# A decoder layer on one core: maxima seven steps ahead of the scores, transposes moved with them

## The chip, the cores and the metric

The kernel runs on one core of a Trainium2 chip. Each of its engines works through its own queue in order: TensorE (PE, matmuls and weight loads), VectorE (DVE), ScalarE (ACT), GpSimd (POOL), and SyncE (SP), which here only issues DMAs. They wait for each other through semaphores. The metric is the device time of one execution in microseconds (us); lower is better.

## What is computed

The reference is one decoder layer on x of shape (8, 512, 256), with 16 heads of 16 features: self-attention with rotary embedding, cross-attention to a context of the same shape, and a mixture of experts, each with a residual sum and a layer norm behind it. Cut to what matters here:

```python
attn = jnp.einsum('bhtd,bhsd->bhts', q, k) * scale
attn = jax.nn.softmax(attn, axis=-1)
out = jnp.einsum('bhts,bhsd->bhtd', attn, v)
x = _layernorm(x + _L0_attn_ref(x, Wqkv, Wout))
x = _layernorm(x + _L0_xattn_ref(x, ctx, ctx, ...))
x = _layernorm(x + _L0_ffn_ref(x, ...))
```

The softmax needs the maximum of each query's scores before the exponential.

## The kernel before

The program has two phases, attention and then the mixture of experts (MoE). Only the attention phase is touched.

**Halves and steps.** For each batch element k (batch, from here on) there is a FIRST half, with the self-attention of batch k, and a SECOND half, with the cross-attention of batch k − 1. The 16 heads are four groups of four (NG = 4), and the 512 keys are four blocks (TT = 4). A half has 16 steps (STEPS): step s takes group s // 4 and block s % 4 of the keys. In a step TensorE does four scores (L721, `ps_sc`, keys on the partitions, queries along the row), four maxima products (L707, `ps_max`, queries on the partitions) for work that is some steps ahead, in the middle the outputs of the step before (`head_outputs`, L738, `ps_out`), and after the last of the four the step's jobs. ScalarE takes the exponentials of the scores (L478). VectorE takes the maxima (L520), negated, into `nm`, one column for each head and query block.

**How a maximum reaches the scores.** Sixteen columns of `nm` make a group. The job `nm0` g (self) or `nm1` g (cross) transposes them on TensorE (L693) into a job bank. ScalarE copies the high part to `mst` (L390), VectorE takes the difference as the low part (L502), and SP writes both by four DMAs into two rows of `qk` on the side of the queries (`mrows`, L229). There they meet rows of ones on the side of the keys, so the scores' product has the maximum already subtracted. The first score of group g, in step 4g, waits for these DMAs (`mrow_in`).

**What else runs in the steps.** The table TASKS gives, for each half and step, the jobs as (kind, number, offset of the batch): projections (`q`, `k`, `v` of the next self-attention, `cq`, `ck`, `cv` of the next cross-attention), transposes of outputs (`ot`, `nt`), output projections (`w0`, `w1`), layer norms (`ln0`, `ln1`), splits (`x`, `c`, `xt`). TensorE does a job at the end of its step; ScalarE and VectorE do their part of it at the start of the next step, VectorE ahead of that step's four maxima. The order inside a step is that of the list.

**Two job banks.** The jobs of TensorE share two PSUM banks in turn, by their place in ORDER, the list of all jobs of both halves. `free_bank` (L629) makes a job wait until the one two places ahead of it has been read out of its bank.

**How far ahead.** LEAD says how many steps the maxima run ahead of the scores. Near the end of a half they belong to the next attention:

```python
inst, first = (cur, TT * (s + LEAD)) if s + LEAD < STEPS else (nxt, TT * (s + LEAD - STEPS))
return [(inst, n) for n in range(first, first + TT)] if inst else []
```

```python
def bank(kind, n):
    return ps_job[:, [t[:2] for t in ORDER].index((kind, n)) % 2, :]
```

```python
at = [t[:2] for t in ORDER].index((kind, n)) - 2
...
pe.wait_ge(read[prev], upto(prev, b, m))
```

**SP's order.** `qk` holds one attention; group g of the next is loaded over it by twelve DMAs (`stack`, L258) when group g of the present one has its scores: for groups 0, 1 and 2 at the end of steps 4, 8 and 12, for group 3 at the start of the next half. The rows come from scratch in HBM: `hbm_ck` and `hbm_cq` are stored in step 3 of FIRST, when `ck` 1 and `cq` 1 are split, and `hbm_self` in steps 3 and 5 of SECOND. In a step SP first issues the `mst` DMAs of that step's `nm` job, then stores, then a `stack`.

Of the kernel before, what the change touches and what calls it, by code (L numbers as in the profile page):

```python
# [18 lines left out]
NG = H // HG  # L19
HM = H // FC  # L20
NSC, NMX = 2, 3
LEAD = 6
PV_AT = 2
JOB_AT = 3
STEPS = NG * TT
# [15 lines left out]
SELF, CROSS = 0, 1  # L41
TASKS = {
    FIRST: {
# [5 lines left out]
    },  # L49
    SECOND: {  # L50
# [5 lines left out]
    },  # L56
}

# [25 lines left out]
def attention_phase(nc, x, xT, cT, w_att, tables, b_cols, bo_rows, x2, hbm_self, hbm_ck, hbm_cq, slots_x, sums):  # L84
    with ExitStack() as ctx:
# [107 lines left out]
        def maxima_of(s, cur, nxt):  # L193

            inst, first = (cur, TT * (s + LEAD)) if s + LEAD < STEPS else (nxt, TT * (s + LEAD - STEPS))
            return [(inst, n) for n in range(first, first + TT)] if inst else []
# [1488 lines left out]
```

## Time and profile before

| | us |
|---|---|
| median of 3 runs | 1755.08 |
| lowest, highest of them | 1749.54, 1757.05 |
| the profiled execution | 1748.39 |
| its span, first to last instruction | 1746.6 |
| TensorE busy with matmuls | 1493.3 (85%) |
| VectorE, ScalarE, GpSimd busy | 1118.8, 913.1, 437.9 |
| mean granted TensorE clock | 0.855 |

The attention phase fills the span up to some 1290 us, MoE the rest. Busy time of TensorE is modelled at the ends of matmuls, so 85% is not 85% of its peak. The granted clock is a share of full speed: 1.00 is 2.4 GHz, 0.50 is 1.2 GHz, and a figure between them is a stretch that has both. In the timeline a row is a run of like instructions: start, length, engine, line, operation, output <- input, count, and in brackets the idle time of the engine before it and what ended that.

### The profile page before, as it was taken

What the parts mean: (1) busy time and instruction counts of PE and PEld (TensorE: products, weight loads), DVE (VectorE), ACT (ScalarE), POOL (GpSimd) and SP (SyncE); (2) the same over time, 40 slices, a digit from 0 to 9 for tenths busy, and PEclk for the clock granted to TensorE, in tenths of its full rate; (3) what the DMA queues carried; (4) which work ended last, traced back from release to release, by engine and by line L of the source; (5) the groups of instructions that cost most, each with busy time, mean ns of one, the idle gap of its engine ahead of it and who ended that gap; (6) DMA issues with size and microseconds to landing.
All of it is one profiled execution on the core that took longest, in us unless ns stands there. A gap on an engine that the chain in (4) does not pass through costs nothing. (4 is left out here: it accounts for less than half of the span.)

```text
span 1746.6 us, 27669 instructions
## 1 busy us (share of the span) xinstructions
PE 1493.3 (85%) x8424; PEld 872.5 (50%) x8424; DVE 1118.8 (64%) x2282; ACT 913.1 (52%) x1702; POOL 437.9 (25%) x411
## 2 busy tenths in 40 slices
PE   3887889989889898988997988886876889999994
PEld 2324334435444444443443533333235778999984
DVE  3716568778678678868877876835514754555556
ACT  3441556656556555655665665651533543555544
POOL 4004013013013003202301301001002543666664
PEclk8657879989888899999998988986557988999998
DMA  4213333333243234233323313204003533677672
GB/s 148 73 53 103 123 94 100 103 110 107 63 130 122 57 109 125 79 118 111 100 98 107 114 50 121 66 1 131 4 1 135 183 128 121 125 148 134 129 202 97
DMA packets 110136, 179.85 MB, mean 103 GB/s; under 512 B 20288, under 2 KB 65984, under 8 KB 107968
## 3 DMA queue, kind: packets, MB, share of 16 engines
q1 hardware_dynamic: 95424, 159.11, 29.3%
q0 software_dynamic: 14592, 19.41, 6.4%
q8 instruction: 42, 0.69, 0.2%
q14 instruction: 78, 0.64, 0.1%
HBM read 98.09 MB, written 79.30 MB: 102 GB/s over the span
## 5 line engine op out<-in xcount | busy, mean ns | idle before, releaser
L520 DVE TENSOR_REDUCE nm<-ps_max 128x1 f32<-128x512 f32 x1024 | 644.7, 682 | 212.3 <-PE ps_max L707 210.9
L478 ACT ACTIVATE prob<-ps_sc 128x512 f32<-128x512 f32 x1024 | 555.8, 596 | 398.2 <-PE ps_sc L721 396.3
L721 PE MATMUL ps_sc<-qk 50*128 50x512 f32 x1024 | 446.1, 520 | 118.4 <-DMA qk<-mst 97.9
L707 PE MATMUL ps_max<-qk 48*128 48x512 f32 x1024 | 466.5, 534 | 26.8 <-DVE nm L520 18.5
L721 PEld LDWEIGHTS ps_sc<-qk 50*128 50x128 f32 x1024 | 185.6, 212 | 479.2 <-ACT prob L478 279.2
L738 PE MATMUL ps_out<-prob,va 128*32 128x512 f32 x2048 | 327.8, 717 | 4.8 <-ACT prob L478 3.4
L707 PEld LDWEIGHTS ps_max<-qk 48*128 48x128 f32 x1024 | 190.8, 212 | 75.4 <-DVE nm L520 63.0
L1472 PE MATMUL ps_gu<-x2f,we 128*128 128x256 f32 (+1 forms) x1344 | 222.1, 320 | 4.6 <-ACT sg L1137 2.4
L1472 PEld LDWEIGHTS ps_gu<-x2f,we 128*128 128x128 f32 x1344 | 189.3, 191 | 21.9 <-DVE h L1363 3.1
L360 POOL TENSOR_TENSOR rstd<-mv,eps 128x2 f32<-128x2 f32 x32 | 6.3, 197 | 680.7 <-DVE mv L589 680.7
L1472 PE MATMUL ps_dn<-we,hf 128*128 128x256 f32 x864 | 123.1, 299 | 11.1 <-DVE totals L1446 10.5
L1472 PEld LDWEIGHTS ps_dn<-we,hf 128*128 128x128 f32 x864 | 117.1, 205 | 12.7 <-DVE hf L1367 12.1
L625 PE MATMUL ps_job<-xf,w 128*128 128x512 f32 x288 | 93.0, 467 | 21.8 <-POOL xf L335 16.7
L738 PEld LDWEIGHTS ps_out<-prob,va 128*32 128x32 f32 x2048 | 43.3, 115 | 99.1 <-issue 92.8
L625 PE MATMUL ps_job<-w,cf 128*128 128x256 f32 x576 | 84.6, 299 | 5.3 <-DVE cf L504 3.6
L1061 POOL DMA_INDIRECT slots_x<-x2in,scat x64 | 65.7, 1026 | 87.3 <-DVE tok L1353 29.5
L625 PEld LDWEIGHTS ps_job<-xf,w 128*128 128x128 f32 x288 | 60.5, 225 | 47.5 <-issue 29.0
L625 PEld LDWEIGHTS ps_job<-w,cf 128*128 128x128 f32 x576 | 75.5, 200 | 15.3 <-issue 8.8
L344 POOL TENSOR_TENSOR res<-res,trig 128x512 f32<-128x512 f32 x32 | 40.9, 1279 | 159.0 <-DVE res L537 159.0
L1075 POOL DMA_INDIRECT sums<-ys,dest x40 | 62.2, 1555 | 49.7 <-DVE dest L1404 26.4
L1075 POOL DMA_INDIRECT x<-ys,dest x40 | 62.1, 1552 | 31.3 <-ACT ys L1202 20.0
L335 POOL TENSOR_TENSOR xf<-raw,xf 128x1024 fp32r<-128x1024 f32 x8 | 19.1, 2389 | 163.1 <-ACT xf L390 163.1
(145 smaller groups left out, 1489.0 us busy)
## 6 DMA issues: line engine op xcount, KB each, us to landing
qk<-hbm_self SPq DMA_DIRECT2D x384, 64.0 KB, 2.3
hbm_self<-stage SPq DMA_DIRECT2D x16, 1024.0 KB, 3.9
qk<-hbm_cq SPq DMA_DIRECT2D x192, 64.0 KB, 2.4
qk<-hbm_ck SPq DMA_DIRECT2D x192, 64.0 KB, 2.3
slots_x<-zeros SPq DMA_DIRECT2D x8, 1360.0 KB, 5.8
xs<-slots_x SPq DMA_DIRECT2D x40, 272.0 KB
weraw<-w_moe SPq DMA_DIRECT2D x11, 768.0 KB
hbm_ck<-stage SPq DMA_DIRECT2D x8, 1024.0 KB, 4.3
```

Source lines behind the costliest of these rows:

```text
L335: nc.gpsimd.tensor_tensor(out, value, high.bitcast(F32), ALU.subtract).then_inc(lo_done[kind], 1)
L344: nc.gpsimd.tensor_tensor(rot[:, c, :], rot[:, c, :], trig[:, 1, :], ALU.mult) \
L360: nc.gpsimd.tensor_tensor(rstd[:, at, :], mv[:, at, 1:2], eps[:, at, :], ALU.add) \
L478: nc.scalar.activation(prob[:, s % 2, j, :], ps_sc[:, (HG * s + j) % NSC, :], ACT.Exp, scale=HD ** -0.5).then_inc(exp_done[a], 1)
L520: nc.vector.tensor_reduce(nm[:, g % 2, r:r + 1], ps_max[:, n % NMX, :], axis=AX.X, op=ALU.max, negate=True).then_inc(max_done[a], 1)
L625: ins = nc.tensor.matmul(out, l(a), r(b), start=(n == 0 and k == 0), stop=(n == len(pairs) - 1 and k == len(parts) - 1))
L707: nc.tensor.matmul(ps_max[:, n % NMX, :], qk[rows, 0, pair, P * c:P * c + P], qk[rows, 1, pair, :], start=True, stop=True).then_inc(smax_d ...
L721: nc.tensor.matmul(ps_sc[:, n % NSC, :], qk[rows, 1, h // 2, P * c:P * c + P], qk[rows, 0, h // 2, :], start=True, stop=True).then_inc(st_ ...
L738: ins = nc.tensor.matmul(ps_out[32 * j:32 * j + 32, :], va[:, a, c, HG * g + j, :], prob[:, s % 2, j, :], start=(c == 0), stop=(c == TT - ...
L1061: nc.gpsimd.indirect_dma_start(rows_x, bass.IndirectOffsetOnAxis(ap=scat[:, q, c, t:t + 1], axis=0), xin[:, q, t, :], None, bounds_check=P ...
L1075: nc.gpsimd.indirect_dma_start(x2 if j // NCH else sums, bass.IndirectOffsetOnAxis(ap=dest[:, c, t:t + 1], axis=0), ys[:, c, t, :], None, ...
L1472: ins = nc.tensor.matmul(o, l(a), r(b), start=(n == 0 and k == 0), stop=(n == len(pairs) - 1 and k == len(parts) - 1))
```

## The change

LEAD goes from 6 to 7: in each step the maxima products and maxima are those that came one step later before. All eight `nm` jobs move one step earlier with them, and stand first in their step's list: from steps 2, 6, 10 and 14 to 1, 5, 9 and 13. Nothing is computed otherwise, and no instruction is added or taken away. What a job bank a job has, and which job it waits for, follows from the new ORDER.

```diff
-LEAD = 6
+LEAD = 7
...
-        0: [("cq", 0, -1), ("ck", 0, -1)], 1: [("ot1", 0, -2), ("cq", 1, -1)], 2: [("nm0", 1, 0), ("ot1", 1, -2)],
...
+        0: [("cq", 0, -1), ("ck", 0, -1)], 1: [("nm0", 1, 0), ("ot1", 0, -2), ("cq", 1, -1)], 2: [("ot1", 1, -2)],
...
-        0: [("q", 0, 1)], 1: [("ot0", 0, 0), ("k", 0, 1), ("qf", 0, 1)], 2: [("nm1", 1, -1), ("ot0", 1, 0)],
...
+        0: [("q", 0, 1)], 1: [("nm1", 1, -1), ("ot0", 0, 0), ("k", 0, 1), ("qf", 0, 1)], 2: [("ot0", 1, 0)],
```

TensorE, in the loop over the batches, FIRST half: the jobs at the end of step 1, before. `cq_read` and the like are the semaphores that say a bank has been read out; `xf,w` is the job `cq` 1, `ident,ot` the job `ot1` 0.

```order
L707 MATMUL ps_max<-qk 128x512 [waits max0]
L640 REGISTER_ALU
L678 MATMUL ps_job<-ident,ot 128x128 [waits oev1,cq_read]
L678 MATMUL ps_job<-ident,ot 128x128 x3
L625 MATMUL ps_job<-xf,w 128x512 [waits xt_read,ck_read]
L625 MATMUL ps_job<-xf,w 128x512 x5
```

The same place in the changed kernel (its lines are one lower):

```order
L706 MATMUL ps_max<-qk 128x512 [waits max0]
L692 MATMUL ps_job<-ident,nm 16x128 [waits max0,cq_read]
L677 MATMUL ps_job<-ident,ot 128x128 [waits oev1,ck_read]
L677 MATMUL ps_job<-ident,ot 128x128 x3
L639 ISA
L624 MATMUL ps_job<-xf,w 128x512 [waits xt_read,nm0_read]
L624 MATMUL ps_job<-xf,w 128x512 x5
```

The transposition of the maxima has come in from step 2, and `cq` 1 waits for the read-out of it in place of that of `ck` 0.

SP's queue in the SECOND half, from the first store of the next self-attention's stage in step 3 on, before:

```order
L300 DMA hbm_self<-stage 128x2048
L258 DMA qk<-hbm_self 16x2x512 x12
L300 DMA hbm_self<-stage 128x2048
L229 DMA qk<-mst 1x8x128 x4
L258 DMA qk<-hbm_self 16x2x512 x12
```

And in the changed kernel:

```order
L299 DMA hbm_self<-stage 128x2048
L257 DMA qk<-hbm_self 16x2x512 x12
L228 DMA qk<-mst 1x8x128 x4
L299 DMA hbm_self<-stage 128x2048
L257 DMA qk<-hbm_self 16x2x512 x12
```

The four `mst` DMAs of group 2 now stand ahead of the second store, and as before behind the twelve loads of group 0 of the next attention.

## Rows read from the trace of the kernel before

**Rows 1.** The waits, whole span: engine, line, releaser: us, times, longest.

```profile
PE ps_sc L721 <- DMA qk<-mst: 97.9, 57, 4.8
```

**Rows 2.** Timeline, TensorE: first scores of a group that waited, one batch.

```profile
604.99 0.50 PE L721 MATMUL ps_sc<-qk 50*128 50x512 f32 x1 [2.80 <-DMA qk<-mst]
...
624.69 0.47 PE L721 MATMUL ps_sc<-qk 50*128 50x512 f32 x1 [0.21 <-DMA qk<-mst]
...
642.77 0.79 PE L721 MATMUL ps_sc<-qk 50*128 50x512 f32 x1 [3.55 <-DMA qk<-mst]
...
660.92 0.47 PE L721 MATMUL ps_sc<-qk 50*128 50x512 f32 x1 [0.73 <-DMA qk<-mst]
...
676.43 0.50 PE L721 MATMUL ps_sc<-qk 50*128 50x512 f32 x1 [2.15 <-DMA qk<-mst]
...
728.45 0.47 PE L721 MATMUL ps_sc<-qk 50*128 50x512 f32 x1 [2.53 <-DMA qk<-mst]
```

**Rows 3.** Timeline, TensorE: outputs of some steps, one in each step.

```profile
527.21 1.93 PE L738 MATMUL ps_out<-prob,va 128*32 128x512 f32 x8
...
531.84 1.93 PE L738 MATMUL ps_out<-prob,va 128*32 128x512 f32 x8
...
600.22 1.07 PE L738 MATMUL ps_out<-prob,va 128*32 128x512 f32 x8
...
605.74 1.11 PE L738 MATMUL ps_out<-prob,va 128*32 128x512 f32 x8
...
669.36 1.06 PE L738 MATMUL ps_out<-prob,va 128*32 128x512 f32 x8
...
672.54 1.06 PE L738 MATMUL ps_out<-prob,va 128*32 128x512 f32 x8
...
677.16 1.06 PE L738 MATMUL ps_out<-prob,va 128*32 128x512 f32 x8
...
724.18 1.07 PE L738 MATMUL ps_out<-prob,va 128*32 128x512 f32 x8
...
729.23 1.73 PE L738 MATMUL ps_out<-prob,va 128*32 128x512 f32 x8
```

**Rows 4.** Stretches: busy of each engine, then granted clock, DMA share, GB/s.

```profile
518.00:534.00 16.00, 15.48 (x60) 4.82 (x61) 10.66 (x19) 7.91 (x16) 4.86 (x5) 0.50 0.58 177
...
605.00:611.00 6.00, 6.00 (x25) 3.56 (x26) 2.57 (x4) 3.09 (x6) 0.00 (x0) 0.72 0.46 126
...
674.00:682.00 8.00, 5.85 (x28) 2.82 (x24) 3.86 (x6) 3.75 (x7) 0.00 (x0) 0.79 0.42 99
682.00:726.00 44.00, 42.87 (x270) 21.98 (x269) 38.97 (x78) 28.77 (x56) 17.07 (x16) 1.00 0.30 97
726.00:737.00 11.00, 8.29 (x36) 2.96 (x36) 6.79 (x14) 6.01 (x12) 2.36 (x1) 0.69 0.30 73
```

**Rows 5.** Timeline, SP's DMA queue: a store, first load, two `mst` issues.

```profile
626.72 0.61 SPq L296 DMA_DIRECT2D hbm_cq<-stage  x1
...
633.10 0.81 SPq L258 DMA_DIRECT2D qk<-hbm_cq  x2
...
638.78 2.82 SPq L229 DMA_DIRECT2D qk<-mst  x4
...
724.51 2.67 SPq L229 DMA_DIRECT2D qk<-mst  x4
```

**Rows 6.** Timeline, VectorE and TensorE: jobs at the end of steps 1, 2.

```profile
613.41 2.48 DVE L520 TENSOR_REDUCE nm<-ps_max 128x1 f32<-128x512 f32 x4
614.58 0.66 PE L678 MATMUL ps_job<-ident,ot 128*128 128x128 f32 x4
614.99 1.65 PE L625 MATMUL ps_job<-xf,w 128*128 128x512 f32 x6
...
619.23 0.28 PE L693 MATMUL ps_job<-ident,nm 128*16 128x128 f32 x1
...
620.46 0.27 DVE L502 TENSOR_TENSOR mst<-ps_job,mst 16x128 fp32r<-16x128 f32 x1
```

13 rows, old and new, of the table TASKS are left out of this document.

## The prediction, made before the change was run

> **What bounds the kernel now.** I read the waits first. They put 97.9 us in 57 waits on one pair: TensorE's scores (L721) against the DMA that writes the negated maxima from `mst` into the rows of `qk` [rows 1]. The attention stage is a chain of steps on TensorE, so such a wait counts in full where nothing else is late. Second, the timeline of TensorE over one batch, 600 to 741 us, says which groups wait [rows 2]. In the FIRST half (self-attention) group 0 waits 2.80, group 1 0.21, group 2 3.55 and group 3 0.73 us; in the SECOND half (cross-attention) group 0 waits 2.15 and group 3 2.53. Third, the idle time in those rows is more than the loss, since a step has idle time anyway. The distance between the output matmuls (L738) of neighbouring steps is the better measure [rows 3]: 3.18 us from 669.36 to 672.54, with no wait and next to no other job. It is 5.52 us into the FIRST half's step 0 (600.22 to 605.74), 4.62 into the SECOND half's (672.54 to 677.16), and 5.05 into its step 12 (724.18 to 729.23).
>
> Fourth, the granted clock by stretches [rows 4]. It is 1.00 (2.4 GHz) in the 44 us from 682, where no wait is long, and 0.69 in the 11 us from 726, which begin with the wait of 2.53 us. It is 0.72 from 605 to 611 and 0.79 from 674 to 682, again behind waits. So a wait is paid twice: as idle time, and as a spell at 1.2 GHz behind it. At 1.2 GHz a step takes 4.63 us (527.21 to 531.84 [rows 3]) against 3.18, so a us there loses 1 − 3.18/4.63 = 0.31 us.
>
> **Part 1, one more step of lead.** Today the last maximum of a group falls three steps ahead of its scores and its transposition two ahead; both move one step earlier, so the distance between the two stays. From the transposition on there is this chain. The DVE part (0.27 us at 620.46) follows the step's maxima [rows 6], then four DMA issues take 2.67 us (724.51) [rows 5], and the scores start 1.27 us after the last issue (728.45 against 727.18) [rows 2, 5]. That is 4.2 us from the DVE part on, against a step of 3.2 to 3.3: late by design wherever the last step before a group has no jobs. One step more is at least 3.18 us, above every one of the losses in rows 3 (2.34, 1.44 and 1.87 us).
>
> What is gained by place, per batch: FIRST group 0, 5.52 − 3.18 = 2.34; SECOND group 0, 4.62 − 3.18 = 1.44; SECOND group 3, 5.05 − 3.18 = 1.87; FIRST group 3, 0.73, and group 1, 0.21 (their idle times, as bounds from above). Sum 6.6 us. **FIRST group 2 (3.55 us) gains nothing.** Its DMAs stand on SP behind the twelve loads of the next attention's group 0, and these wait for the stores of `stage`: store of `hbm_cq` issued at 626.72, first load at 633.10, `mst` only at 638.78, when the twelve are out [rows 5]. In the new order the `mst` DMAs still stand behind the same twelve loads, however early the maxima are ready. What the wait hangs on is the job `ck` 1, a step 3 job, and that does not move.
>
> The clock behind the waits that go: (1 − 0.72) × 6 / 0.5 = 3.4 us at 1.2 GHz, (1 − 0.79) × 8 / 0.5 = 3.4, and (1 − 0.69) × 11 / 0.5 = 6.8; together 13.6 us × 0.31 = 4.2 us. A batch thus gives 6.6 + 4.2 = 10.8 us. The waits of one batch in rows 2 add to 12.0 of the 97.9 us, so the trace holds some eight batches' worth. Six batches have both attentions in full. The first, the last and the self-attention of batch 7 run alone or half alone, mostly at the lower clock, and I take them as one batch together. 7 × 10.8 = **76 us gained**.
>
> **Part 2, the job banks.** The jobs use two PSUM banks in turn, by their place in ORDER, and a job waits until the one two places before it has been read out. Moving `nm0` 1 and `nm1` 1 to step 1 makes three jobs there, in both halves, so the third (`cq` 1, `k` 0) waits for the transposed maxima right before it in the same step. The order of the changed kernel shows the wait: `nm0_read` on the first matmul of `cq` 1, where `ck_read` stood. What it costs comes from rows 6. The step's four maxima end at 613.41 + 2.48 = 615.89; the DVE part of `nm` takes 0.27, so the bank is free at 616.16 and `cq` 1 can start at some 616.25. It started at 614.99: 1.26 us later. Scores of step 2 stand behind it on TensorE, exps and maxima behind those, so nothing hides it. The SECOND half has the same build (`q` 0 in step 0, `k` 0 third) and is taken alike. Both jobs are there in FIRST for batches 1 to 7 and in SECOND for 1 to 6: 13 × 1.26 = **16 us lost**. Of it TensorE idles 616.25 − (614.58 + 0.28 + 0.66) = 0.7 us a time. Elsewhere the two banks stay one step apart; I went through ORDER for this. The other steps with two jobs are as before.
>
> Will a gap of 0.7 us take the clock down? Behind FIRST group 3's wait of 0.73 us it did in one batch, 16 us at 0.50 from 518 [rows 4], and did not behind the wait at 660.92 [rows 2]. So the bound is from 0 to 16 × 0.31 = 5 us a time. The steps around step 1 are full of jobs, unlike step 12, so I take one in ten: 0.5 us a time, 13 times, **6 us lost**. The Trainium skill, page "TensorE: Matmul & The Clock Gate", section "A second HAM failure mode: psum-queue depth-cycling", warns of just this kind of short idleness between groups of matmuls that cycle through banks, as something that lets the clock oscillate. By that rule each of the 13 gaps would be followed by a spell at the lower clock, the fourth case below; the trace of before has no such gap in step 1, so it can't say yet.
>
> **Part 3, the ramps and SP.** Before batches 0 and 1's first scores and the last cross-attention, 28 maxima run alone in place of 24. Four more at some 0.62 us (2.48 / 4) are 2.5 us a time. Twice the `mst` wait there covers them (their DMAs are on their way meanwhile); between nothing and 7.4 us, I take **3 us lost**. On SP two things change places: `mst` of SECOND group 2 now goes ahead of the second store to `hbm_self` (2.7 us later), and `mst` of cross group 0 ahead of the store of `res`. Neither has a reader that is near: group 2 of the next self-attention is loaded seven steps on. The maxima also need their rows of `qk` one step earlier. Twelve loads take 5.5 to 7.4 us to issue from steps 4, 8, 12 and 0, and the maxima begin in steps 9, 13, 1 and 5. Five steps are over 16 us, so nothing is lost. MoE is untouched.
>
> **Sum.** 76 − 16 − 6 − 3 = 51 us. The profiled execution took 1748.39 us (span 1746.6), which gives 1697 for one like it. It is at the fast end of the four times shown, so I take the sum off the median: 1755.1 − 51 = 1704, rounded to 1703.
>
> **Rivals.**
> 1. Forecast, 1703 (1686 to 1722): chance 0.60.
> 2. The waits go but the clock does not come back: the lower level follows other gaps (the new ones, FIRST group 2's). Gain 7 × 6.6 = 46, less 16 and 3: 1755 − 27 = 1728 (1722 to 1742). For it: the wait of 0.73 us that was enough at 518. Against it: 44 us at 1.00 once no wait comes. 0.17.
> 3. More comes back: batches 0 and 7, now at 1.2 GHz for long, stay at 2.4, some 25 us more: 1678. 0.08.
> 4. **Slower**: each new gap in step 1 takes TensorE to 1.2 GHz for as long as at 518, 5 + 1.26 us, 13 times = 81, and the clock gain is gone. 1755 − 46 + 81 + 3 = 1793. Without the clock gain it turns slower once more than 5 of the 13 gaps do so ((46 − 16 − 3) / 5). 0.08.
> 5. The lead does nothing: every group's `mst` DMAs are held on SP as group 2's are, and only the costs stay: 1755 + 16 + 3 = 1774. Against it: at 724.51 they are issued right after the DVE part, with SP idle before. 0.03.
>
> The rest, 0.04, lies between cases 2 and 4, about no change. The range 1676 to 1738 takes in cases 1 and 3 and most of 2. A measurement of this kernel tells 0.5% (9 us) from no change: faster 0.85 (cases 1 to 3), same 0.04, slower 0.11 (cases 4 and 5).
>
> **What would show it.** Waits of L721 on `qk<-mst` fall from 97.9 to some 30 us, nearly all FIRST group 2 at 3.5 us each; a new wait of TensorE's job matmuls (L624 in the new numbering) on the DVE part of `mst`, 13 times at 0.7 us. Granted clock over the span above 0.855, with the low spells only behind FIRST group 2. Distance into steps 0 and 12 near 3.2 to 3.5 us. I am wrong if the `mst` wait stays in groups 0 and 3, if the clock falls after step 1, or if a wait on `stack_in` or on DVE takes the place in steps 9 to 13.

## The result, and the profile after

| us | before | after |
|---|---|---|
| median, lowest to highest | 1753.72, 1749.54 to 1757.05 (4 runs) | 1686.44, 1682.61 to 1698.08 (4 runs) |
| the profiled execution | 1748.39 | 1687.87 |
| its span | 1746.6 | 1686.0 |
| mean granted TensorE clock | 0.855 | 0.891 |

The ratio is 0.963, with a 95% interval from 0.958 to 0.968: faster by 67 us, where 52 were forecast. The changed program was run once more among the experiments below, 1675.39 us against 1753.27, ratio 0.957 (0.954 to 0.960): faster by 78 us. I call the two sets the first and the second. Runs more than 1.5% above the fastest of their kernel are left out of the ratios but not of the medians; only the kernel with three edits together has such runs, two of its six. Line numbers after the change are one lower: scores L720, maxima products L706, outputs L737, transposition L692, jobs L624, the low part of `mst` L501, maxima L519, its DMAs L228.

The busy times and the clock by slices, of the page of after:

```profile
PE 1458.2 (86%) x8424; PEld 864.6 (51%) x8424; DVE 1116.5 (66%) x2282; ACT 913.2 (54%) x1702; POOL 438.3 (26%) x411
...
PEclk8596899999989988988997998985958879999997
```

The work is the same. TensorE's busy time is 35 us shorter with the same 8424 matmuls, since fewer of them ran at 1.2 GHz. The waits of TensorE over the whole span, which answer to [rows 1] (engine, line, releaser: us, times, longest):

```profile
PE ps_sc L720 <- ACT prob L477: 44.0, 89, 1.1
PE ps_sc L720 <- DMA qk<-mst: 26.8, 9, 4.7
...
PE ps_job L624 <- DVE mst L501: 11.3, 13, 1.3
```

The wait for the `mst` DMAs fell from 97.9 us in 57 waits to 26.8 in 9. Seven of the nine are FIRST group 2 (3.5 to 4.7 us each); the other two have 0.2 and 0.35 us. The new wait of the job matmuls for the read-out of the transposed maxima is there 13 times. Its timeline in the FIRST half's step 1, and next to it the wait of group 2 that stayed (start, length, and in brackets the idle time before and what ended it):

```profile
581.42 1.67 PE L624 MATMUL ps_job<-xf,w 128*128 128x512 f32 x6 [0.84 <-DVE mst L501]
```

```profile
609.09 0.79 PE L720 MATMUL ps_sc<-qk 50*128 50x512 f32 x1 [3.60 <-DMA qk<-mst]
```

The same batch's stretches, which answer to [rows 4] (busy of PE, PEld, DVE, ACT, POOL, then granted clock, DMA share, GB/s):

```profile
577.00:607.00 30.00, 27.20 (x171) 13.85 (x170) 23.16 (x43) 19.35 (x37) 0.00 (x0) 1.00 0.37 130
607.00:619.00 12.00, 9.91 (x39) 3.65 (x40) 5.41 (x10) 5.10 (x10) 0.00 (x0) 0.58 0.24 67
619.00:635.00 16.00, 14.36 (x87) 6.76 (x86) 14.35 (x29) 10.20 (x20) 7.07 (x9) 1.00 0.51 158
635.00:649.00 14.00, 12.47 (x46) 3.95 (x46) 8.72 (x15) 5.85 (x12) 0.00 (x0) 0.54 0.22 68
649.00:714.00 65.00, 61.06 (x372) 30.32 (x368) 54.98 (x107) 43.86 (x84) 19.41 (x17) 0.99 0.30 92
```

The stretch that holds the new gap in step 1 (581.42) is at 1.00: the gap of 0.84 us did not take the clock down. The fall from 607 is that of FIRST group 2, as forecast. The fall from 635 was not forecast: it comes in the FIRST half's step 13, behind this:

```profile
631.68 2.96 POOL L368 TENSOR_TENSOR x1b<-x,bo 128x256 f32<-128x256 f32 x4
...
632.05 2.73 DVE L597 TENSOR_SCALAR res<-res,mv,rstd 128x256 f32<-128x256 f32 x4
...
635.44 0.50 PE L706 MATMUL ps_max<-qk 48*128 48x512 f32 x1 [1.17 <-DVE nm L519]
```

VectorE's four layer norm operations take 2.73 us beside GpSimd's `x1b`, the maxima come late, and TensorE idles 1.17 us in the `qk` products. This wait stands in five of the seven FIRST halves of the loop; in the other two the norm and `x1b` do not meet. Before, the same pair of rows and a wait of 1.09 us stood in this step:

```profile
667.74 0.49 PE L707 MATMUL ps_max<-qk 48*128 48x512 f32 x1 [1.09 <-DVE nm L520]
```

There the clock stayed up: the next two outputs are 3.18 us apart (669.36 and 672.54 in [rows 3]).

**Step by step.** For a clean comparison I take one FIRST and the following SECOND half from the changed kernel's second profiled execution, in which this batch has no fall in step 13. Its outputs, one row a step, from step 0 of the FIRST half to step 1 of the SECOND, which answer to [rows 3]:

```profile
559.44 1.07 PE L737 MATMUL ps_out<-prob,va 128*32 128x512 f32 x8
565.95 1.06 PE L737 MATMUL ps_out<-prob,va 128*32 128x512 f32 x8
571.81 1.07 PE L737 MATMUL ps_out<-prob,va 128*32 128x512 f32 x8
...
591.31 1.07 PE L737 MATMUL ps_out<-prob,va 128*32 128x512 f32 x8
598.12 1.93 PE L737 MATMUL ps_out<-prob,va 128*32 128x512 f32 x8
602.86 1.07 PE L737 MATMUL ps_out<-prob,va 128*32 128x512 f32 x8
...
626.29 1.06 PE L737 MATMUL ps_out<-prob,va 128*32 128x512 f32 x8
629.80 1.07 PE L737 MATMUL ps_out<-prob,va 128*32 128x512 f32 x8
633.72 1.07 PE L737 MATMUL ps_out<-prob,va 128*32 128x512 f32 x8
```

The distances between such rows, the same halves before and after, in us:

| distance between outputs | before | after | gained | forecast |
|---|---|---|---|---|
| into FIRST step 0 | 5.52 | 3.52 | 2.0 | 2.34 |
| FIRST steps 1 to 4 (sum) | 17.26 | 18.23 | -0.97 | -1.26 |
| into FIRST step 8 (group 2) | 7.10 | 6.81 | 0.3 | 0 |
| into FIRST step 12 | 3.94 | 3.57 | 0.4 | 0.73 |
| into SECOND step 0 | 4.62 | 3.51 | 1.1 | 1.44 |
| the step behind it | 5.43 | 3.92 | 1.5 | clock |
| SECOND steps 1 to 4 (sum) | 17.40 | 18.07 | -0.67 | -1.26 |
| into SECOND step 12 | 5.05 | 3.17 | 1.9 | 1.87 |
| the two steps behind it | 8.76 | 6.90 | 1.9 | clock |

The FIRST and SECOND half together took 140.8 us before and 133.4 after: 7.5 us for a clean batch, against 10.8 − 2 × 1.26 − 2 × 0.5 = 7.3 by the prediction's terms.

**By halves, whole attention phase.** The 13 halves in the middle sum to 923.1 us before, 891.1 after (870.9 in the second execution). Each is taken from its step 1 to the next half's step 1. The six SECOND halves went from 427.5 to 392.0 us (390.2 in the second execution), but the seven FIRST halves from 495.6 to 499.0 (480.7): in the first execution the falls in step 13, and longer spells at the lower clock behind group 2, took back all that the FIRST halves had gained. The three at the ends (the first, which holds the ramp of batch 1; the one up to the last cross-attention; that attention alone) sum to 303.6 before, 271.5 after (280.3 in the second). What lies outside the attention steps, nearly all of it MoE, took 3.5 us more after (1.5 in the second). That is 32 + 32 − 3.5 = some 60 us in the first execution, and 52 + 23 − 1.5 = some 74 in the second.

### The profile page after: what moved, and what is told of

It reads as the page before. It is cut to its first block and busy times, and to the rows that moved or that the text cites. A ratio compares the mean times of both kernels' runs of the same rounds, so it can differ in the third digit from the quotient of the medians.

```text
span 1686.0 us, 27694 instructions
## 1 busy us (share of the span) xinstructions
PE 1458.2 (86%) x8424; PEld 864.6 (51%) x8424; DVE 1116.5 (66%) x2282; ACT 913.2 (54%) x1702; POOL 438.3 (26%) x411
## 5 line engine op out<-in xcount | busy, mean ns | idle before, releaser
L519 DVE TENSOR_REDUCE nm<-ps_max 128x1 f32<-128x512 f32 x1024 | 640.4, 682 | 164.4 <-PE ps_max L706 155.9
L706 PE MATMUL ps_max<-qk 48*128 48x512 f32 x1024 | 466.4, 525 | 40.3 <-DVE nm L519 22.7
L720 PE MATMUL ps_sc<-qk 50*128 50x512 f32 x1024 | 432.2, 494 | 71.4 <-ACT prob L477 44.0
L720 PEld LDWEIGHTS ps_sc<-qk 50*128 50x128 f32 x1024 | 178.1, 201 | 414.6 <-ACT prob L477 286.8
L737 PE MATMUL ps_out<-prob,va 128*32 128x512 f32 x2048 | 305.1, 671 | 5.2 <-ACT prob L477 3.4
L706 PEld LDWEIGHTS ps_max<-qk 48*128 48x128 f32 x1024 | 189.3, 207 | 96.0 <-DVE nm L519 72.8
L624 PE MATMUL ps_job<-xf,w 128*128 128x512 f32 x288 | 83.7, 430 | 28.2 <-POOL xf L334 16.8
L737 PEld LDWEIGHTS ps_out<-prob,va 128*32 128x32 f32 x2048 | 42.4, 112 | 93.2 <-issue 86.1
L624 PE MATMUL ps_job<-w,cf 128*128 128x256 f32 x576 | 84.5, 299 | 3.6 <-DVE cf L503 1.7
L624 PEld LDWEIGHTS ps_job<-w,cf 128*128 128x128 f32 x576 | 75.6, 200 | 9.1 <-issue 4.7
L624 PEld LDWEIGHTS ps_job<-xf,w 128*128 128x128 f32 x288 | 53.9, 200 | 50.7 <-issue 25.9
```

The source lines that it names most:

```text
L519: nc.vector.tensor_reduce(nm[:, g % 2, r:r + 1], ps_max[:, n % NMX, :], axis=AX.X, op=ALU.max, negate=True).then_inc(max_done[a], 1)
L624: ins = nc.tensor.matmul(out, l(a), r(b), start=(n == 0 and k == 0), stop=(n == len(pairs) - 1 and k == len(parts) - 1))
L706: nc.tensor.matmul(ps_max[:, n % NMX, :], qk[rows, 0, pair, P * c:P * c + P], qk[rows, 1, pair, :], start=True, stop=True).then_inc(smax_d ...
L720: nc.tensor.matmul(ps_sc[:, n % NSC, :], qk[rows, 1, h // 2, P * c:P * c + P], qk[rows, 0, h // 2, :], start=True, stop=True).then_inc(st_ ...
L737: ins = nc.tensor.matmul(ps_out[32 * j:32 * j + 32, :], va[:, a, c, HG * g + j, :], prob[:, s % 2, j, :], start=(c == 0), stop=(c == TT - ...
```

## The experiments

Each gives the median of its runs, the ratio to the kernel before on the same chip with its 95% interval, and what its own profile shows. `...` stands for lines left out.

### Which part does it: the lead or the transpositions?

The lead alone, the transpositions left where they were:

```
-LEAD = 6
+LEAD = 7
```

> The kernel before with LEAD 7 and the nm jobs left in steps 2, 6, 10 and 14. My theory: what was late was the chain behind the transposition (DVE part 0.27 us, four DMA issues 2.7 us, 1.3 us to the scores), so the lead alone frees nothing: the waits of L721 on the mst DMAs stay near 98 us and the time within 0.5% of the kernel before, 1745 to 1762 us. Rival: the maxima themselves were late (VectorE held TensorE up at the end of a group), so the lead alone gives a good part of the 67 us: 1700 to 1725 us.

1767.92 us; ratio 1.006 (1.002 to 1.010). The wait is all there:

```profile
PE ps_sc L721 <- DMA qk<-mst: 99.6, 56, 4.3
```

The rows of maxima leave `nm` when the transposition is issued, and this did not move. So an earlier maximum that nothing picks up gains nothing; it costs 0.6%. The three stretches with a ramp are 12 us longer in its profile, so the four more maxima in each, and the clock in them, explain a part; how much, no run separates.

The other half, the changed table of jobs with LEAD 6:

```
-LEAD = 7
+LEAD = 6
```

> The changed kernel with LEAD 6: the nm jobs in steps 1, 5, 9 and 13, but a group's last maximum in the same step as its transposition. My theory: the mst waits go as in the changed kernel, but TensorE stands in front of each of the 64 transpositions until VectorE has taken that step's fourth maximum, some 1.0 to 1.3 us a time: 64 to 83 us lost against the changed kernel, 1735 to 1770 us. Rival, the early transposition is all that counts and the lead is not needed: within 1% of the changed kernel, 1680 to 1703 us.

1780.77 us; ratio 1.011 (1.005 to 1.017): 10 us slower than the upper end of what I had expected. The two waits of its profile:

```profile
PE ps_job L692 <- DVE nm L519: 78.0, 64, 1.4
...
PE ps_sc L720 <- DMA qk<-mst: 18.9, 7, 4.2
```

The `mst` wait goes just as in the changed kernel, which shows that the place of the transposition decides it. But each of the 64 transpositions now stands in TensorE's queue ahead of the scores and waits 1.2 us on average for VectorE to finish the group's last maximum. Moved together, neither wait is left. The effect belongs to neither part alone.

### What does the third job in step 1 cost?

Group 1's transpositions back in step 2, so that the third job of step 1 has its bank free:

```
-... 1: [("nm0", 1, 0), ("ot1", 0, -2), ("cq", 1, -1)], 2: [("ot1", 1, -2)],
+... 1: [("ot1", 0, -2), ("cq", 1, -1)], 2: [("nm0", 1, 0), ("ot1", 1, -2)],
-... 1: [("nm1", 1, -1), ("ot0", 0, 0), ("k", 0, 1), ("qf", 0, 1)], 2: [("ot0", 1, 0)],
+... 1: [("ot0", 0, 0), ("k", 0, 1), ("qf", 0, 1)], 2: [("nm1", 1, -1), ("ot0", 1, 0)],
```

> The changed kernel with nm0 1 and nm1 1 back in step 2, so that no step has three bank jobs; all else as changed. My theory: the 13 waits of the third job on the read-out of the maxima (0.84 us idle each, 1.26 us of delay each) go, and group 1's mst wait of 0.2 to 0.9 us comes back: 16 us less 3: 10 to 16 us faster than the changed kernel, 1670 to 1677 us. Rival: the delay is taken up elsewhere (by the fixed chain to FIRST group 2 and by VectorE), so removing it changes nothing, 1683 to 1690 us.

1680.74 us (1676.32 to 1690.52); ratio 0.954 (0.949 to 0.959), beside 1686.44 and 1675.39 in the changed kernel's two sets: above what I had expected, and inside the spread between those two. The profile shows why it isn't a clean removal of the cost: the group 1 waits come back.

```profile
PE ps_sc L720 <- DMA qk<-mst: 34.9, 25, 4.3
```

In most halves these are 0.2 us each, but 1.59 and 2.18 in the cross-attentions of batches 6 and 7. The time of this kernel says nothing on the size of the third job's cost; its step lengths do. Its outputs in step 1 and step 5 of one FIRST half:

```profile
586.87 1.06 PE L737 MATMUL ps_out<-prob,va 128*32 128x512 f32 x8
...
604.16 1.06 PE L737 MATMUL ps_out<-prob,va 128*32 128x512 f32 x8
```

That is 17.29 us for steps 1 to 4. Over all halves of the loop the mean is 17.17 us in FIRST and 17.35 in SECOND; the kernel before has 17.17 and 17.34, the changed kernel 18.12 and 18.09. So the whole loss in these steps, 0.95 us in FIRST and 0.76 in SECOND, hangs on the place of group 1's transposition and goes with it.

The other way round: the transpositions stay in step 1, and the third job goes to step 2.

```
-... 1: [("nm0", 1, 0), ("ot1", 0, -2), ("cq", 1, -1)], 2: [("ot1", 1, -2)],
+... 1: [("nm0", 1, 0), ("ot1", 0, -2)], 2: [("cq", 1, -1), ("ot1", 1, -2)],
-... 1: [("nm1", 1, -1), ("ot0", 0, 0), ("k", 0, 1), ("qf", 0, 1)], 2: [("ot0", 1, 0)],
+... 1: [("nm1", 1, -1), ("ot0", 0, 0), ("qf", 0, 1)], 2: [("k", 0, 1), ("ot0", 1, 0)],
```

> The changed kernel with its third bank job of step 1 moved to step 2 (cq 1 in FIRST, k 0 in SECOND): two jobs in each, nothing else. It measures the new wait by itself, without bringing group 1's mst wait back. My theory: the 13 waits on the read-out of the maxima go. Against steps 1 to 4 of the kernel before, the changed one loses 0.6 to 0.75 us a half and not 1.26, since VectorE has less to do in step 2: 8 to 12 us faster than the changed kernel. Rival: my first figure, 16 us, or nothing, because VectorE is as far behind either way.

1671.77 us (1655.65 to 1679.24); ratio 0.954 (0.951 to 0.957), 3.6 us under the changed kernel's second set, where I had expected 8 to 12; the intervals overlap, so by time the two are not told apart. The wait for the read-out of `mst` is gone. Steps 1 to 4 of the FIRST half take 17.51 us against 18.23, which is 0.72 less; those of the SECOND take 18.06 against 18.07. So the wait itself is removed, and the steps get back about half of its price: 6 of 11 us, all in FIRST halves. What ends last in step 2 with two jobs is not shown.

### What does FIRST group 2 wait for?

SP issues the twelve loads for group 0 of the next attention in step 4, and their data hang on a store of `stage`. Here they go in one step later, behind the `mst` DMAs of group 2, in FIRST halves alone:

```
-                    if nxt and s % TT == 0 and s:
+                    if nxt and s == (TT + 1 if h == FIRST else TT):
+                        stack(nxt, last, 0)
+                    if nxt and s in (2 * TT, 3 * TT):
                         stack(nxt, last, s // TT - 1)
```

> The changed kernel with one change on SP: in the FIRST half the twelve loads of the next attention's group 0 are issued in step 5, behind the mst DMAs of group 2, and no longer in step 4 ahead of them. My theory: FIRST group 2 waits only because of that order; its seven waits of 3.5 to 4.7 us go, with the low clock of 6 to 10 us behind each: 25 us of waits and some 20 us of clock, 1635 to 1655 us. Rival: the waits are bound by something else (the read-out of the maxima, the DMA itself), and stay: 1680 to 1692 us. Second rival: the loads come too late for the maxima of step 9 and a wait on stack_in of like size takes the place: 1680 to 1700 us.

1640.75 us (1640.07 to 1653.87); ratio 0.934 (0.928 to 0.941). SP's queue and TensorE's waits:

```profile
583.35 2.77 SPq L228 DMA_DIRECT2D qk<-mst  x4
586.44 0.81 SPq L257 DMA_DIRECT2D qk<-hbm_cq  x2
```

```profile
PE ps_max L708 <- DMA qk<-hbm_ck: 12.3, 7, 8.9
...
PE ps_sc L722 <- DMA qk<-mst: 2.1, 3, 1.5
```

The `mst` DMAs of group 2 are issued at 583.35 and the loads behind them, from 586.44. The wait of 26.8 us is down to 2.1, and the step in which it stood takes 3.2 us in place of 6.8 to 7.2. In its place comes a wait of 0.4 to 1.0 us on the loads' data in six of the seven FIRST halves; the one of 8.9 us is at the last ramp, where the changed kernel has it too (9.3, and 6.2 before). The time lies in the range of the first theory. This shows what the prediction had read from [rows 5]: group 2's wait comes from a place in SP's queue, which the longer lead did not move.

### Does the clock fall because of the wait?

The wait of FIRST group 2 stays, but TensorE is kept busy in it: twelve matmuls of 512 columns into a free job bank, whose result nobody reads, at the end of step 7 for batches 2 to 7. They are added work.

```
+                            if h == FIRST and s == 7 and cur and exists(k - 2):
+                                free_bank("nt1", 1, k)
+                                for r in range(12):
+                                    nc.tensor.matmul(bank("nt1", 1), w[:, HI, 0, 0:P], w[:, HI, 0, 0:T],
+                                                     start=True, stop=True)
```

> The changed kernel with twelve more matmuls of 512 columns at the end of step 7 of each FIRST half that has a later batch's jobs (batches 2 to 7), into the free job bank, on constant weights; nothing reads them. They fill some 2.6 us of TensorE's wait for FIRST group 2's mst DMAs (3.5 us) and are work without use. It takes the two prices of a wait apart. My theory: the clock falls behind a wait because TensorE is idle in it; filled, the same wait leaves the clock at 1.00 in steps 8 to 10, which at 1.2 GHz take 5.2, 4.6 to 5.6 and 4.65 us and otherwise 3.95 to 4.7: six times 1.5 to 2.5 us, 8 to 15 us faster than the changed kernel although it does more. Rival: the fall hangs on something else (the DMAs, the time since the last fall), it stays, and the kernel is as fast as the changed one or up to 5 us slower.

1666.73 us (1650.39 to 1671.25); ratio 0.952 (0.950 to 0.954), half a per cent under the 0.957 of the changed kernel's second set, with intervals that just touch. The filler, the scores behind it and the stretch after them:

```profile
596.19 2.98 PE L765 MATMUL ps_job<-w 128*128 128x512 f32 x12
...
600.06 0.49 PE L720 MATMUL ps_sc<-qk 50*128 50x512 f32 x1 [0.89 <-DMA qk<-mst]
```

```profile
600.00:612.00 12.00, 11.57 (x73) 5.83 (x74) 9.70 (x19) 7.60 (x15) 0.89 (x2) 1.00 0.23 68
```

The scores start no earlier, since the DMAs set them, but they run at once at 2.4 GHz: 0.49 us, where they took 0.79 behind the bare wait at 609.09. Clock 1.00 behind it against 0.58 from 607 to 619. The step behind takes 3.56 to 3.63 us in all six batches (4.4 to 5.2 in the changed kernel). So the low spell hangs on TensorE's own idleness, and not on the DMA or on time. This is the clearest evidence that a wait here is paid twice. By the ratios the gain is some 9 us, in the range of the theory. The fall in step 13 stays in two halves of this profile.

### Where does the fall in step 13 come from?

First, the changed kernel again, to see what two executions of one program share:

> The changed kernel once more, unaltered, beside the next three. In its first profile the granted clock fell in step 13 of four of the seven FIRST halves that hold both attentions (steps of 4.8, 4.6 and 5.2 us where 4.4, 3.2 and 3.5 stand otherwise). If that belongs to the kernel, it falls again in at least three; if it was chance, in none or one. Time 1683 to 1698 us.

1675.39 us (1672.47 to 1681.09, 6 runs); ratio 0.957 (0.954 to 0.960). In its profile the fall in the FIRST half's step 13 comes in one half of seven, where the first execution had four. I had expected at least three. A half with the fall takes 74.5 us, one without 67.8, but not all of the 6.7 us is the fall: from step 13 on the distances are 4.83, 4.63, 5.17 and 5.13 us in the first execution and 4.52, 3.17, 3.51 and 3.92 for the same half in the second, which is 4.6 us; the other 2.1 lie in the distances into steps 8 to 10, at the wait of group 2 and in the spell behind it. So chance decides in this step, and three falls more are 14 us of the 20 by which the loops of the two executions differ. The two profiled executions as a whole differ by 13.5 us, since the first had the shorter last attention (below).

Then the suspect that the change brought: `nm1` 0, which it moved into step 13, goes back to step 14.

```
-... 13: [("nm1", 0, -1), ("x1b", 0, -1)],
+... 13: [("x1b", 0, -1)], 14: [("nm1", 0, -1)],
```

> The changed kernel with nm1 0 alone back in FIRST step 14. It asks whether the change itself put the fall of the clock into FIRST step 13. Theory A, it did, because that transposition stands behind the layer norm's idle time in the same step: the falls in step 13 go (0 or 1 of 7), but SECOND group 0 waits for its mst DMAs again, 2 us and a fall of the clock behind it: about as fast as the changed kernel, 1678 to 1700 us. Theory B, the idle time behind the layer norm takes the clock down whatever follows it (in the kernel before, the mst wait one step earlier only shifted when): as many falls as in the changed kernel and the wait on top, 1695 to 1712 us.

1694.37 us (1688.64 to 1701.5); ratio 0.967 (0.964 to 0.971). The falls stay (4 of 7), as theory B had it, so the transposition in step 13 is not their cause, and the SECOND half's group 0 waits again:

```profile
PE ps_sc L720 <- DMA qk<-mst: 36.4, 12, 4.6
```

Last, GpSimd's `x1b` goes from FIRST step 13 to SECOND step 0, behind the job `q` 0, away from VectorE's layer norm:

```
-... 13: [("nm1", 0, -1), ("x1b", 0, -1)],
+... 13: [("nm1", 0, -1)],
...
-        0: [("q", 0, 1)], 1: ...
+        0: [("q", 0, 1), ("x1b", 0, -1)], 1: ...
```

> The changed kernel with GpSimd's addition x1b moved from FIRST step 13 to SECOND step 0, behind its part of the job q 0. In the traces VectorE's layer norm in FIRST step 13 takes 2.6 to 2.7 us while x1b runs on GpSimd, and 1.37 us for the same four instructions in SECOND step 12, where GpSimd is idle. Theory: the two share something, so apart from x1b the norm takes 1.4 us, TensorE's idle time of 1.2 us behind it goes, and with it the fall of the clock in FIRST step 13: 7 x 1.2 us and some 4 x 5 us, 15 to 30 us faster than the changed kernel. Rival: the fall has another cause (the transposition of the maxima in that step), then only 5 to 9 us. Second rival: the norm is slow by its own form (it writes over its input) and nothing changes.

1662.95 us (1659.16 to 1678.62); ratio 0.950 (0.946 to 0.954), 12 us under the changed kernel's second set, where I had expected 15 to 30 from some four falls. The layer norm alone:

```profile
634.76 1.37 DVE L597 TENSOR_SCALAR res<-res,mv,rstd 128x256 f32<-128x256 f32 x4
```

1.37 us for the four operations, in place of 2.73. The step takes 3.18 us in place of 4.5 to 4.8, and none of the five halves that had the wait has the fall. Five steps that are 1.3 us shorter are 7 us, and one fall less 4.6: about the 12 that were measured. The pair had cost the kernel before the same 1.3 us a step, without the fall.

### All together

The third job in step 2, the loads behind the `mst` DMAs, and `x1b` late:

> Three of the edits together on the changed kernel: cq 1 and k 0 in step 2, SP's loads of cross group 0 behind the mst DMAs, x1b behind q 0. If their gains add (46, 4 and 12 us below the changed kernel's 1675 to 1686): 1615 to 1630 us, with no wait on mst over 1 us and a clock near 0.93. If they overlap in the clock, of which each gives back a part: 1630 to 1640 us.

1618.92 us (1598.29 to 1628.8); ratio 0.920 (0.916 to 0.924), which is 1611 us against the 1750.76 of the kernel before: in the range for gains that add by the median, and just under it by the ratio. One wait on `mst` is over 1 us, 1.27. Since the SECOND half had gained nothing from the job's move, a last kernel takes it back there and puts `nm1` 1 in step 2, except in the last cross-attention, which runs alone and where group 1 would wait:

```
-... 1: [("nm1", 1, -1), ("ot0", 0, 0), ("qf", 0, 1)], 2: [("k", 0, 1), ("ot0", 1, 0)],
+... 1: [("ot0", 0, 0), ("k", 0, 1), ("qf", 0, 1)], 2: [("nm1", 1, -1), ("ot0", 1, 0)],
...
+            rows = [t for t in TASKS[half].get(s, []) if t != ("nm1", 1, -1)]
+            if s == (1 if isinstance(k, int) and k >= B else 2) and half == SECOND:
+                rows = [("nm1", 1, -1)] + rows
```

> The same, but in SECOND k 0 is back in step 1 and nm1 1 in step 2, as in the kernel before, except for the last cross-attention, which keeps nm1 1 in step 1. By the step lengths, steps 1 to 4 of SECOND take 18.06 us with k 0 in step 2 and 17.33 in the kernel before: 6 x 0.7 = 4 us faster than the one above. If group 1's mst wait comes back in SECOND of batches 7 and takes the clock down there, the two are equal.

1607.67 us (1604.7 to 1627.97); ratio 0.918 (0.916 to 0.920). It beats both kernels: 8.2% under before. Against the one above it is not told apart (the intervals overlap), though its SECOND halves take 64.8 us against 65.6. Group 1's wait did come back in the cross-attention of batch 6 (1.59 us). One batch of its loop and a little more:

```profile
500.00:640.00 140.00, 133.10 (x802) 65.57 (x803) 119.68 (x230) 94.11 (x180) 37.83 (x37) 1.00 0.36 113
```

TensorE is busy for 95% of these 140 us at 1.00 throughout; the low spells that are left lie in the first two halves, at the ends and in MoE.

## Why the prediction held, and where its terms were off

**The path (part 1).** Right, and shown. The chain from transposition to scores was read as 4.2 us against a step of 3.2, and one step more covered it in every group of the loop but FIRST group 2. The gains by place in the table above are 5.4 us a batch where 6.6 were forecast (2.0, 1.1, 1.9 and 0.4). The clock's part is 1.5 + 1.9 = 3.4 us behind SECOND groups 0 and 3, against 4.2 for the batch. FIRST group 2 kept its wait for the reason given; moving the loads took it away.

**The job bank (part 2).** The mechanism was right (13 waits, the third job behind the read-out of the transposed maxima), and so was the idleness: 0.84 us a time, 0.7 forecast. The price was mis-sized: not 1.26 us a time but, by the means over the loop, 0.95 in FIRST and 0.76 in SECOND, so 7 × 0.95 + 6 × 0.76 = 11 us and not 16. The step that failed is "nothing hides it". The sum took the full delay of the job's start, but step 2 has lost its transposition, and part of the delay is caught up behind it: in FIRST the distance from step 1 to 2 grew by 1.15 us (4.71 to 5.86), close to the forecast, and that from 3 to 4 shrank by 0.50 (4.90 to 4.40), while that from 4 to 5 grew by 0.38. With the transposition back in step 2 all four distances return to those of before. Why the later steps share the loss in this way is not shown.

**The clock behind the new gap.** I took one in ten at 5 us, 6 us in all. None was seen: step 2 and those behind it have the lengths of 2.4 GHz in all loop halves of both executions. The Trainium skill, page "TensorE: Matmul & The Clock Gate", section "A second HAM failure mode: psum-queue depth-cycling", gives short idleness between groups that cycle through banks as a cause of oscillation. It speaks of idleness that comes in each iteration and often; here one gap of 0.84 us comes in 65 to 75 us, and none of the 13 took the clock down. The prediction's reading, that each single gap would do so (rival 4), was too strong, and the page's own case is not tested here. The idleness of 1.17 us in step 13, which stands in five halves, was followed by the lower clock in four of them in one execution and in one in the other.

**The clock where no wait was looked at.** The fall in FIRST step 13 was not in the sum at all. It cost 4 × 4.6 = 19 us in the first profiled execution and 5 in the second. What made it likelier than in the kernel before, where a wait of 1.09 us stood and the clock stayed, is open: the transposition in step 13 is not it. The traces narrow it a little. The kernel before and the one with the lead alone both still wait for group 3's `mst` DMAs in the step ahead, and in neither is the wait on VectorE, which their profiles have three and four times at the full clock, followed by a fall; with group 3's wait gone the falls come, in one to four halves of five. That the one keeps off the other is not tested.

**The ends.** The three halves at the ends were taken as one batch's worth less the ramps, 10.8 − 3 = 8 us. They gave 32 and 23. This is the term that was off most, and rival 3 had named its mechanism (batches 0 and 7 stay at 2.4 GHz, some 25 us). The self-attention of batch 0, with the ramp behind it, gave 11.5 and 15.7 us, the cross-attention of batch 6 with its ramp 4.6 and 8.6, that of batch 7 16.0 and −1.0. (The prediction lists the self-attention of batch 7 here in place of the cross-attention of batch 6; it runs in full company, 67.6 and 67.9 us.) The 3 us for the ramps were not seen: the three together took 1.2 us more in the first execution and 1.0 less in the second, although the maxima's waits for their loads in them grew from 7.9 to 17.2 and 15.7 us. The last cross-attention of the first and of the second execution of the same kernel:

```profile
1173.00:1224.00 51.00, 43.38 (x215) 13.03 (x213) 21.02 (x36) 33.86 (x66) 0.00 (x0) 0.87 0.04 10
```

```profile
1145.00:1212.00 67.00, 61.07 (x213) 17.38 (x211) 20.97 (x35) 33.22 (x66) 0.00 (x0) 0.50 0.02 6
```

The same matmuls, at 0.87 in 51 us and at 0.50 in 67 us. Both executions enter at the lower level, with steps of 4.56 us. In the first the clock rises after three steps, which then take 3.10 to 3.25 us; in the second it never does. What decides is not shown, so this 17 us is luck in a single profile and only the median over runs can be told.

**The sum.** In the loop 6 × 10.8 − 16 − 6 = 43 us were forecast; 32 and 52 came. With the ends (8 forecast, 32 and 23) that makes the forecast 52 against 67. The errors had both signs: too dear a job bank and too little for the ends, against the fall in step 13. That they cancelled in part is luck, and so is the room to the edge: the first set, 1686.44 us, lies at the fast end of the forecast's own case (1686 to 1722), and the second, 1675.39, is 0.6 us outside the whole range (1676 to 1738), near rival 3's 1678. Of the others, the `mst` wait did not stay in groups 0 and 3 (rival 5), and step 1 stayed at full clock (rival 4). Rival 2, a clock that falls at other places, is out as a whole, since the clock came back in the SECOND halves, but the falls in step 13 are a part of it.

## What to carry to other kernels

A prefetch distance is the distance of its whole chain: the lead alone (ratio 1.006) and the hand-over alone (1.011) each left the kernel slightly slower, and together they gave 0.963 or less. Before moving a step, follow each instruction of it to its queue. FIRST group 2's wait was a place on SP, and a change there of three lines brought more (1640.75 us) than the third job had ever cost. And price a wait with the clock spell behind it: filling a wait with useless matmuls, which shortens nothing by itself, took 0.8 to 1.7 us off the step behind it in each of six batches.

## What the hardware showed that I had not expected

**Two engines on one tile memory.** VectorE's `tensor_scalar` on 128x256 f32 takes 0.40 us alone and up to 0.83 beside GpSimd's `tensor_tensor`. All 32 of that form (minimum, median, maximum in ns; start of first and last), in the changed kernel and in the one with `x1b` late:

```profile
L597 DVE TENSOR_SCALAR res<-res,mv,rstd x32: 381/516/827, 356.3 to 1245.4; 128x256 f32<-128x256 f32 x32
```

```profile
L597 DVE TENSOR_SCALAR res<-res,mv,rstd x32: 382/408/412, 367.0 to 1225.6; 128x256 f32<-128x256 f32 x32
```

GpSimd's own operation takes 0.77 to 0.80 us where it starts beside the norm and 0.72 to 0.76 in the kernel with `x1b` late, so nearly all of the delay falls on VectorE. The two run in step: around 632 us GpSimd's operations start at 632.37, 633.12 and 633.86, and VectorE's 0.11 to 0.12 us behind each, one every 0.74 us, where alone they start every 0.32. The Trainium skill, page "SBUF — State Buffer", section "SBUF: two separate sides", says that the pair of ports that the two engines share is locked for a whole instruction and not split. It says so of a VectorE operation in a two-port mode or with two inputs in SBUF, and which of them this one would be, no run here shows; VectorE's pace of one operation for each of GpSimd's agrees with a lock, and does not prove it.

**The clock has memory and luck.** One program, on one input, took 74.5 or 67.8 us for a FIRST half and 67 or 51 for the last attention, with the granted clock as the difference that the traces show. Two executions of the changed kernel, 1687.87 and 1674.36 us, differ by more than some of the edits tried here are worth.

**What stays open.** Why a wait of 1.1 to 1.2 us in step 13 takes the clock down in some halves and not in others, and why the kernel before was spared in that step. The experiments show only that with the collision of `x1b` and the layer norm gone there is neither the wait nor the fall: in none of the three kernels that have `x1b` late.
